# Attention blocks of 128 score groups on one core: the score buffers and the ring of exponential slots run on over the block boundary

## The reference

```python
q, k, v = split(x @ qkv_w + qkv_b)          # per head
q, k = rot(q), rot(k)
scores = einsum('bhqd,bhkd->bhqk', q, k) / 4
attn = softmax(scores)
out = einsum('bhqk,bhkd->bhqd', attn, v) @ out_w + out_b
x = layernorm(x + out)
n = layer_norm(x, g1, be1);  x = x + n + (n @ mix_w + mix_b)
n = layer_norm(x, g2, be2)
y = sum over the 2 best experts of  p_e * (silu(n @ w1[e] + b1[e]) @ w2[e] + b2[e])
return layernorm(x + y)
```

## Time and profile before

| | |
|---|---|
| time, median of 3 runs (lowest, highest) | 1675.38 us (1675.26, 1676.09) |
| time of the profiled execution | 1675.51 us |
| its span | 1673.8 us |
| PE busy | 1610.3 us (96% of the span) |
| ACT busy | 1244.0 us (74%) |
| exponentials (L1300) | 1024, ACT busy 955.7 us with them |
| ACT idle just before them | 34.8 us, of that 33.4 us until PE's scores |
| instructions | 45794 |

### The profile page before, as it was taken

How to read it: one execution, slowest core, us unless ns; L and a number is a source line. 1 busy time by engine, 2 the same in 40 slices (tenths; PEclk the granted TensorE clock), 3 DMA queues, 4 the chain that set the end, 5 groups by cost and what they waited for, 6 DMA issues and landing times.

```text
span 1673.8 us, 45794 instructions
## 1 busy us (share of the span) xinstructions
PE 1610.3 (96%) x17936; PEld 916.9 (55%) x17941; DVE 536.7 (32%) x1443; ACT 1244.0 (74%) x1869; POOL 469.3 (28%) x495
## 2 busy tenths in 40 slices
PE   7989999999999999999999999999999999999990
PEld 5543333433433433433433433358999999999990
DVE  4551125435435425525525535526210000000004
ACT  5659999999999999999999999963444444444441
POOL 4630011112102202202202212115455444444441
PEclk9999999999999999999999999999999999999995
DMA  5776310101103442301100101646668766666645
GB/s 166 205 155 90 64 40 15 48 26 34 50 24 69 89 81 52 100 28 31 50 28 30 51 26 34 241 143 169 182 175 225 198 185 166 186 186 186 176 119 207
DMA packets 108487, 181.18 MB, mean 108 GB/s; under 512 B 14121, under 2 KB 80361, under 8 KB 108137
## 3 DMA queue, kind: packets, MB, share of 16 engines
q1 hardware_dynamic: 95010, 160.88, 33.2%
q0 software_dynamic: 13296, 17.77, 5.6%
HBM read 134.07 MB, written 40.18 MB: 104 GB/s over the span
## 4 chain that ended last, share of the span: by engine, by line
PE 81%; ACT 4%; issue 4%; DVE 1%; DMA 1%; POOL 0%; POOLq 0%; ACTq 0%; DVEq 0%
PE at_s L1385 24%; PE at_po L1397 23%; PE at_s L1511 14%; PE at_s L1524 14%; ACT place L1300 4%; PE at_small L1413 4%; PE at_small L1406 1%; PE at_po L1500 1%; DMA rows_out<-place,at_v 1%; DVE cb_ln_stats L696 1%; DVE place L1750 0%; POOL place L1254 0%; DMA place<-rows_out 0%; POOL place L1259 0%; DVE at_v L1714 0%
## 5 line engine op out<-in xcount | busy, mean ns | idle before, releaser
L1300 ACT ACTIVATE place<-at_s 128x1024 f32<-128x1024 f32 x1024 | 955.7, 1154 | 34.8 <-PE at_s L1385 33.4
L1385 PE MATMUL at_s<-place 99*32 99x512 bf16 x8192 | 575.3, 381 | 12.7 <-ACT place L1300 7.6
L1397 PE MATMUL at_po<-place,at_v 128*32 128x512 f32 x4096 | 531.7, 594 | 0.0
L1385 PEld LDWEIGHTS at_s<-place 99*32 99x32 bf16 x8192 | 195.0, 95 | 485.6 <-issue 220.2
L1511 PEld LDWEIGHTS at_s<-ex_xT,place 128*128 128x128 f32 x2272 | 264.3, 192 | 5.9 <-issue 1.7
L1317 ACT ACTIVATE place<-at_s,b_turned 128x128 f32<-128x128 f32 x568 | 161.6, 368 | 142.2 <-PE at_s L1511 141.5
L1511 PE MATMUL at_s<-ex_xT,place 128*128 128x128 f32 x2272 | 265.7, 275 | 0.0
L1524 PE MATMUL at_s<-place 128*128 x1136 | 257.0, 379 | 1.1 <-ACT place L1317 0.6
L1524 PEld LDWEIGHTS at_s<-place 128*128 128x128 f32 x1136 | 210.4, 190 | 27.3 <-issue 1.6
L1397 PEld LDWEIGHTS at_po<-place,at_v 128*32 128x32 f32 x4096 | 125.3, 111 | 104.4 <-issue 1.2
L1333 ACT ACTIVATE place<-at_s,at_v 128x256 f32<-128x256 f32 x71 | 33.6, 474 | 162.2 <-PE at_s L1524 156.9
(11 more groups left out here) (216 smaller groups left out, 950.9 us busy)
## 6 DMA issues: line engine op xcount, KB each, us to landing
place<-in_w SPq DMA_DIRECT2D x79, 1024.0 KB, 5.5
place<-k_parts SPq DMA_DIRECT2D x48, 256.0 KB, 5.4
place<-q_parts SPq DMA_DIRECT2D x192, 64.0 KB
at_v<-rows_in SPq DMA_DIRECT2D x71, 129.0 KB, 2.1
place<-in_x SPq DMA_DIRECT2D x8, 512.0 KB, 4.5
at_heads_T<-at_o SPq DMA_DIRECT2D x128, 32.0 KB
rt_x_in<-in_x SPq DMA_DIRECT2D x8, 512.0 KB, 4.1
rows_out<-rt_total SPq DMA_DIRECT2D x8, 512.0 KB, 5.0
```

What stands on the lines that cost most here:

```text
L1300: nc.scalar.activation(probs[:, slot(n), :], p_s[n % BUFFERS][:, :], ACT.Exp).then_inc(exp_done, 1)
L1385: last = nc.tensor.matmul(p_s[n % BUFFERS][j:j + 32, s * 512:(s + 1) * 512], k_rows[0:ROWS_M, quad(q).start + h, kt * P + j:kt * P + j + 3 ...
L1397: last = nc.tensor.matmul(p_o[32 * h:32 * h + 32, :], v_one[q % 2][:, h, kt, :], probs[:, slot(q * NG + g), s * 512:(s + 1) * 512], start= ...
```

## The change

There is now one count over all blocks: group n of block i takes buffer (128 i + n) mod 3 and slot (128 i + n) mod 6. With this the buffers come free in the order in which the next block's groups follow, and PE issues them as 0, 1, 2; `FIRST`, `scored_before` and `held_before` fall away. ACT waits at every group for that group's own scores and for the round that reads the group six before. The expert stage takes for `p_h` and `p_y` the buffers that come free in the same order as before: `p_h` were `at_s0` and `at_s1` and are now `at_s2` and `at_s0`; `p_y` was `at_s2` and is now `at_s1`. No matmul, exponential, copy or DMA is added or taken away.

```diff
--- before.py
+++ after.py
@@ -767,7 +767,6 @@
     NB = UNITS * NG
     NR = UNITS * KT
     LEAD = 2 * KT
-    FIRST = (2, 0, 1)
     JOBS = 10
     OUT_AT = {14: (0, 0), 16: (0, 2), 18: (1, 0), 20: (1, 2)}
     NORM_AT = {48: 0, 52: 1}
@@ -775,7 +774,6 @@
     SENT_AT = {80: 0, 84: 1}
     ROUTER_AT = {88: 0, 90: 4}
     COUNT_AT = 118
-    assert NB % RING == 2 and NB % BUFFERS == 2
     with ExitStack() as stack:
         m = Mem(nc, stack)
 
@@ -848,8 +846,9 @@
         y = room[:, y_at:y_at + 2 * D].rearrange("p (u n) -> p u n", u=2)
         biased = room[:, y_at + 2 * D:y_at + 3 * D]
         rows_now = v_one[0][:, :, :, :].rearrange("p h a w -> p (h a w)")[:, 0:XR * ROW].rearrange("p (r n) -> p r n", r=XR)
-        p_h = [p_s[u][:, 0:FC * P].rearrange("p (s n) -> p s n", s=FC) for u in range(2)]
-        p_y = [p_s[2][:, u * 512:u * 512 + D] for u in range(2)]
+        AFTER = GROUPS * NB
+        p_h = [p_s[(AFTER - 2 + u) % BUFFERS][:, 0:FC * P].rearrange("p (s n) -> p s n", s=FC) for u in range(2)]
+        p_y = [p_s[AFTER % BUFFERS][:, u * 512:u * 512 + D] for u in range(2)]
         p_x = p_o[:, 0:KC * P].rearrange("p (s n) -> p s n", s=KC)
         p_x_first = small[:, :].rearrange("p (t s n) -> p t s n", t=2, s=KC)
 
@@ -930,24 +929,19 @@
         SEND_ROUNDS = {0: (3, 5, 8, 10, 13, 15), 1: (18, 21)}
         ROUTER_AFTER, SEND_AFTER = 10, 15
 
-        def slot(n):
-
-            return n % RING if n < NB - 2 else n % RING + 2
-
-        def held_before(n):
-
-            earlier = [m for m in range(n) if slot(m) == slot(n)]
-            return earlier[-1] if earlier else max(m for m in range(NB) if slot(m) == slot(n)) - NB
+        def slot(i, n):
+
+            return (i * NB + n) % RING
+
+        def scores(i, n):
+
+            return p_s[(i * NB + n) % BUFFERS]
 
         def rounds_reading(n):
 
             before = 0 if n >= 0 else NR
             n = n % NB
             return (n // NG) * KT + n % NG // PAIR + 1 - before
-
-        def scored_before(n):
-
-            return {0: 2, 1: 3, 2: 1}.get(n, n + 1)
 
         def rounds_at(g):
 
@@ -1294,10 +1288,10 @@
             def _(act):
                 def exponentials(i, routed):
                     for n in range(NB):
-                        act.wait_ge(scored, i * NB + scored_before(n) + 2 * NG)
-
-                        act.wait_ge(weighed, i * NR + rounds_reading(held_before(n)) + LEAD)
-                        nc.scalar.activation(probs[:, slot(n), :], p_s[n % BUFFERS][:, :], ACT.Exp
+                        act.wait_ge(scored, i * NB + n + 1 + 2 * NG)
+
+                        act.wait_ge(weighed, i * NR + rounds_reading(n - RING) + LEAD)
+                        nc.scalar.activation(probs[:, slot(i, n), :], scores(i, n)[:, :], ACT.Exp
                                              ).then_inc(exp_done, 1)
                         if routed and n == 104:
                             router(i - 1)
@@ -1376,13 +1370,13 @@
                 def score(i, n):
 
                     q, g = n // NG, n % NG
-                    if g == 0 or n == 2:
+                    if g == 0:
                         pe.wait_ge(loaded_k[q], (i // QC) * (16 * 6) + 16 * (6 if q == 0 else 7))
                         pe.wait_ge(loaded_q[q % 2], i * (2 * 16 * 7) + (q // 2 + 1) * (16 * 7))
                     for s in range(PAIR):
                         kt, h = (g * PAIR + s) // QUAD, (g * PAIR + s) % QUAD
                         for j in range(0, P, 32):
-                            last = nc.tensor.matmul(p_s[n % BUFFERS][j:j + 32, s * 512:(s + 1) * 512],
+                            last = nc.tensor.matmul(scores(i, n)[j:j + 32, s * 512:(s + 1) * 512],
                                                     k_rows[0:ROWS_M, quad(q).start + h, kt * P + j:kt * P + j + 32],
                                                     q_rows[q % 2][0:ROWS_M, h, :], start=True, stop=True)
                     last.then_inc(scored, 1)
@@ -1395,7 +1389,7 @@
                     for h in range(QUAD):
                         g, s = (kt * QUAD + h) // PAIR, (kt * QUAD + h) % PAIR
                         last = nc.tensor.matmul(p_o[32 * h:32 * h + 32, :], v_one[q % 2][:, h, kt, :],
-                                                probs[:, slot(q * NG + g), s * 512:(s + 1) * 512],
+                                                probs[:, slot(i, q * NG + g), s * 512:(s + 1) * 512],
                                                 start=(kt == 0), stop=(kt == KT - 1))
                     last.then_inc(weighed, 1)
 
@@ -1470,7 +1464,7 @@
                         if n + BUFFERS < NB:
                             score(i, n + BUFFERS)
                         elif not is_last:
-                            score(i + 1, FIRST[n + BUFFERS - NB])
+                            score(i + 1, n + BUFFERS - NB)
                         q, g = n // NG, n % NG
                         for kt in rounds_at(g):
                             weigh(i, q, kt)
@@ -1545,7 +1539,7 @@
                 pe.sem_inc(o_copied, 1)
                 pe.sem_inc(small_read, 1)
                 pe.sem_inc(h_ready, 4)
-                for n in FIRST:
+                for n in range(BUFFERS):
                     score(0, n)
                 attend(0, False, False, 0)
                 pe.wait_ge(loaded_w, 16 * 9)
```

## The result

The changed kernel takes 1673.92 us (median of 22 runs, 1671.64 to 1675.22); the kernel before, measured again beside it, 1676.05 us (22 runs, 1674.74 to 1677.09). The medians differ by 2.1 us. The ratio over all runs is 0.9985, 95% interval 0.9979 to 0.9991; by it the change saves 2.5 us, between 1.5 and 3.5, about 0.15% of the time. The forecast was 1673.4 us and a gain of 2.0 us.

What follows compares the result with a forecast made beforehand. ACT's pace of 0.917 us an exponential was taken as the bound; 7 boundaries x 0.28 us gave 2.0 us off the profiled 1675.51, and the runs' median, 0.13 lower, gave 1673.4 us, range 1672.2 to 1675.9.

Steps and rivals of the forecast that it cites:

- The rival that took the starts for the work: At block boundaries, profiled starts show the cost: 0.70 us each, 4.9 us in all, 1670.5 us; chance 0.11.
- Part (1): At each of 7 block boundaries, issuing group 0 at step 125 removes its wait: 0.28 us gained each.
- Part (2): Behind the boundary, no later score group is late; the smallest lead is 0.32 us, at group 7.
- The proof offered from block 0: Its 95 exponentials run over unit starts n = 64 and 96, with the same bunch of rounds, without idle time.
- Parts (3) and (4): Round 0's wait for DVE's copy is hidden by 0.95 us; step 14's products still find their DMAs landed.
- part (4): Step 14's products need four DMAs; they come 0.28 us earlier, with 5.3 us left for the landing.
- Parts (5) to (7): Older slot waits, score order at block 0's start, experts' other buffers: no gain or loss taken; tiles stay 7.25 us.
- the rival of the slower side: In the experts, other PSUM buffers could slow hidden products by 0.20 us a tile: 1687.6 us; chance 0.07.
- No gain: PE hands the boundary's 0.28 us back where ACT next waits for it: 1675.4 us; chance 0.15.

Runs made afterwards that it cites:

- slots_only: Kernel before with only the ring of six slots running on over the block boundary, score buffers and order 2, 0, 1 kept: 1675.72 us, ratio 0.9997.
- order_only: Changed kernel with the slot numbering of before, so only score groups and their buffers run on: 1673.42 us, ratio 0.9983 to the kernel before.
- round_behind: Kernel before, order 2, 0, 1 kept, with the round ahead of group 0's scores issued behind them: 1676.08 us, ratio 1.0002.
- group0_last: Changed kernel with the next block's score groups issued in order 1, 2, 0: 1680.13 us, ratio 1.0023 to the kernel before.
- group1_last: Changed kernel with the next block's score groups issued in order 0, 2, 1: 1673.96 us, ratio 0.9988 to the kernel before.
- turned: Kernel before with only the three PSUM buffers' numbers turned by two, order and slots kept: 1675.91 us, ratio 1.0001.
- filler: Changed kernel with ten unused products added at the end of the projection on PE: 1675.11 us, ratio 0.9996 to the kernel before.

## Why the prediction was right

**What bounds a block.** ACT's pace of 0.917 us by its ends, and only group 0 late by 0.28 us. slots_only and order_only show it from both sides: removing the hold at group 126 gives nothing, removing the wait at group 0 gives everything. The rival that took the starts for the work asked for 2.2 us in slots_only and got 0.3, inside the interval of no change; for the whole change it asked for 4.9 us (5.0, when the starts of the earlier trace rows are summed: 4.33 us over four groups, less 4 x 0.904), outside the measured 1.5 to 3.5.

**Part (1), the order.** The cause given for the wait, scores issued at step 126 behind a round, is shown by round_behind, which moved it by one group, and by group0_last, which made it larger by what the durations say (1.74 us measured, 1.73 expected). The gain of a block measured 0.30 us in the profile, 0.29 of it at the boundary, where 0.28 was forecast: 2.1 us in the sum in place of 2.0.

**Part (2), what is late next.** Nothing is up to group 18. The smallest lead was put at 0.32 us, at group 7. By the single records of the changed kernel, reckoned as in the prediction (end of the scores against the end of the exponential before, less 0.10 us), it is 0.31 us at each of the seven boundaries, and those of groups 0, 1 and 2 are 1.06, 0.69 and 1.06 us, as forecast. That a lead of 0.15 us is enough is shown by group1_last at another group. The proof offered from block 0, a row without idle time, was weaker than it was called, since lateness can hide in such a row: group 19 of block 4 ends 0.13 to 0.14 us late inside one, in both kernels. The ends bear the claim out: from group 34 to 127 of block 0 they are nowhere more than 0.922 us apart in the kernel before.

**Parts (3) and (4), the covers.** They held: copy to product shrank by 0.29 us and no idle time appeared. The 5.3 us that part (4) left for the landing of the DMAs were those of the kernel before; with the product earlier they are 5.0 (623.23 less 615.82 + 2.42), which is still enough.

**Parts (5) to (7), priced at nothing.** Slots: slots_only. Start of block 0: "nothing" was a little too strict, for the order can be worth up to 0.17 us in executions in which PE's clock falls early (last section); in the two profiles compared POOL released the first exponential. Buffer numbers in the experts: turned shows that they cost nothing, and the rival of the slower side falls with it, for a tile stayed at 7.24 us in both.

**No gain**, the rival in which PE hands the time back: group0_last refutes it in the other direction, since its 0.53 us a boundary stayed in full (block lengths of 124.69 us). In the changed kernel itself all seven blocks behind the first are shorter by 0.28 to 0.31 us, measured from the end of one group 127 to that of the next.

**The size.** 2.1 us by the medians and 2.5 (1.5 to 3.5) by the ratio, against 2.0: inside the interval. The blocks of the profile account for 2.1. The 0.4 us between the two measures is not resolved, since single runs of one kernel lie 2 to 4 us apart. The forecast of 1673.4 us lies 0.5 us below the measured median because of its starting point and not of the sum: the kernel before stood at 1675.38 us in its first three runs and at 1676.05 in 22.

## What to carry to other kernels

Where buffers are handed round in a ring and the trip count is no multiple of it, let the index run on over the loop's boundary: it costs only index arithmetic in an unrolled program, and it keeps the order in which a buffer comes free equal to the order in which it is wanted. Whether it pays is another matter: here the slots' ring gave nothing, another order of issue (group1_last) did as well as the plain one, and only one late score group of three had a cost. What such a break costs can be worked out step by step before deciding: for each item, when it is issued, when it is there, and when it is needed. It is the lateness of each item that counts and not the number of waits removed. And price a wait by the distance between ends of the waiting engine's instructions, against the pace of a stretch without idle time; the distance between starts overstated this one by 2.5 times (0.70 us against 0.28).

## What the runs showed of the hardware that was not expected

**A record of ACT can open long before the work.** The same exponential is recorded with 1.016 to 1.659 us in the changed kernel:

```profile
L1294 ACT ACTIVATE place<-at_s x1024: 1016/1166/1659, 117.8 to 1102.7; 128x1024 f32<-128x1024 f32 x171
```

In a stretch without idle time the starts are 0.904 us apart and the ends 0.917, so the record grows by 13 ns each time. A hold shorter than the head start that has built up cost nothing here: order_only held group 126 by 0.30 us when the records were 1.37 us long, 0.35 us over a lone one, and lost nothing by the ends. A longer one cost what was over: in slots_only group 0 starts 1.58 - 0.90 = 0.68 us late, the head start is 1.39 - 1.02 = 0.37, and the ends lose 0.29. The Trainium skill, Perfetto Trace Analysis, section Per-engine timelines, puts the start of such a record where the ALUs begin; the trace does not agree: the same work does not last 1.016 us in one place and 1.659 in another, and in slots_only 0.32 us of delay moved from one start to another and the ends stayed.

**The first exponentials of block 0 take a different time in each profile.** PE stands idle for 3.5 us when the stages change, and its granted clock then is at half (the lower level, 1.2 GHz) for a stretch that begins and ends at another place each time. In turned and in the changed kernel it fell while PE stood idle (at 114.2 and 115.4 us), in the kernel before only at 116.5 us, behind its first 24 matmuls of the stage. The last window with the lower clock in it, in the kernel before, the changed kernel and turned (windows of 2 us; the clock stands before the DMA share):

```profile
122.00:124.00 2.00, 2.00 (x24) 0.68 (x20) 0.00 (x0) 1.04 (x2) 0.00 (x0) 0.67 1.05 123
```

```profile
122.00:124.00 2.00, 2.00 (x24) 0.54 (x20) 0.00 (x0) 2.00 (x3) 0.00 (x0) 0.95 1.03 127
```

```profile
124.00:126.00 2.00, 2.00 (x28) 0.65 (x24) 0.00 (x0) 1.33 (x2) 0.00 (x0) 0.89 1.05 129
```

In the two windows ahead of these all three have 0.50. Group 7 of block 0 starts 10.47 us after ACT's list opens (the row ACT_TABLE_LOAD below) in the profile before, 10.84 us in turned, and 9.31 us in the changed kernel; the rows of ACT of before and of after:

```profile
114.14 1.28 ACT L1345 ACT_TABLE_LOAD   x1 [11.76 <-PEq L609]
...
124.61 23.02 ACT L1300 ACTIVATE place<-at_s 128x1024 f32<-128x1024 f32 x25 [0.46 <-PE at_s L1385]
```

```profile
115.35 1.28 ACT L1339 ACT_TABLE_LOAD   x1 [11.76 <-PEq L609]
...
124.66 23.02 ACT L1294 ACTIVATE place<-at_s 128x1024 f32<-128x1024 f32 x25 [0.27 <-PE at_s L1379]
```

The changed kernel's profile opened the stage 1.2 us later and had caught this up by group 7. That is chance for the most part and not the change, as the other profiles show. Set side by side, group 7 starts the later after the opening, the later the lower clock ends after it:

| kernel | lower clock ends, us after the opening | group 7 starts, us after the opening |
|---|---|---|
| changed kernel | 6.8 | 9.31 |
| order_only | 6.9 | 9.34 |
| filler | 8.1 | 9.91 |
| round_behind | 8.2 | 9.98 |
| before | 9.2 | 10.47 |
| slots_only | 9.5 | 10.72 |
| turned | 9.8 | 10.84 |
| group1_last | 9.8 | 10.83 |

The order of the score groups does not sort them: filler has that of the changed kernel, round_behind that of the kernel before. (group0_last, whose first exponential waits for all three groups, has 9.2 and 11.04.) A small part can be the order: in turned and in slots_only, where the clock had fallen early, the first exponential was released by PE, since it waits for two score groups in the old order; in group1_last, where the clock fell early too but group 0 is issued first, it starts as soon after the opening as in the changed kernel (2.41 us in both), though group 1, issued last, is then 0.11 us late. The row of slots_only:

```profile
116.98 5.61 ACT L1295 ACTIVATE place<-at_s 128x1024 f32<-128x1024 f32 x6 [1.08 <-PE at_s L1380]
```

Its 1.08 us of idle time, and 1.09 in turned, stand against 0.92 where POOL releases it, so the old order can cost up to 0.17 us there. Whether the clock's fall is also what spreads the runs of one kernel is not shown. The times on record speak for a part: of the 60 runs of the kernel before beside the experiments, those with a mean granted clock of 0.986 took 1676.9 us in the mean (5 runs), those with 0.987 took 1676.2 (39) and those with 0.988 took 1675.2 (16), and the filler's 11 runs, the closest together, all have 0.988. But the changed kernel's 22 runs show no such order (1674.1, 1673.2 and 1673.8 us), so it stays open.
